# A four-layer message-passing network on one core: the segment maximum worked inside the pipeline of edge phase 2

## The reference

```python
ms = src_s[edge_src] + dst_s[edge_dst]
mv = src_v[edge_src] + dst_v[edge_dst]
w = h @ rw3 + roff
# products of w1..w5 with ms, mv and the edge direction give ds, dv
ls, lv = _eq_lin(ds, dv, lin_ws, lin_bs, lin_wv)
alpha = ls[:, :H * A].reshape(e, H, A)
a = jnp.einsum('ehk,hk->eh', _smooth_leaky(alpha), alpha_dot)      # 8 scores an edge
amax = jax.lax.stop_gradient(jax.ops.segment_max(a, edge_dst, num_segments=n))
a = jnp.exp(a - amax[edge_dst])
a = a / (jax.ops.segment_sum(a, edge_dst, num_segments=n)[edge_dst] + 1e-12)
ns = jax.ops.segment_sum(vs * a[..., None], edge_dst, num_segments=n)
```

## Time and profile before

| | |
|---|---|
| median of 3 runs | 6494.27 us (6494.11 to 6495.6) |
| profiled execution | 6489.29 us, span 6487.5 us |
| PE busy | 5139.3 us (79%) |
| POOL busy | 4415.7 us (68%) |
| DVE busy | 4269.7 us (66%) |
| ACT busy | 2869.0 us (44%) |
| granted TensorE clock | 0.913 of 2.4 GHz |

### The profile page before, as it was taken

The page is one execution under the profiler, slowest core; times in us unless marked ns, Lnnn a source line. Parts: engine busy times, 40 slices in busy tenths (PEclk is TensorE's granted clock), DMA queues, the critical chain, the costliest instruction groups (busy, mean ns, idle before and its releaser), DMA issues. The chain is left out here.

```text
span 6487.5 us, 124927 instructions
## 1 busy us (share of the span) xinstructions
PE 5139.3 (79%) x28257; PEld 3947.1 (61%) x28280; DVE 4269.7 (66%) x14852; ACT 2869.0 (44%) x6302; POOL 4415.7 (68%) x4689
## 2 busy tenths in 40 slices
PE   8899966669997997999655344438999989998676
PEld 6566656646666995677322134337888867776666
DVE  3566658854544886888677521217888878776788
ACT  5333347744443664444200000006777764443566
POOL 8688856658886897766377688875666657887222
PEclk9899989989998998999888766669999999999999
DMA  8566667746665763555311244443333324554665
GB/s 318 126 123 125 121 153 221 220 106 131 130 126 148 232 229 120 166 158 157 115 34 32 76 85 77 74 56 99 110 106 111 105 91 88 88 85 68 223 223 188
DMA packets 592231, 850.72 MB, mean 131 GB/s; under 512 B 220782, under 2 KB 340382, under 8 KB 587566
## 3 DMA queue, kind: packets, MB, share of 16 engines
q1 hardware_dynamic: 409646, 693.65, 33.6%
q0 software_dynamic: 182400, 154.98, 17.3%
HBM read 469.53 MB, written 377.54 MB: 131 GB/s over the span
## 5 line engine op out<-in xcount | busy, mean ns | idle before, releaser
L1140 POOL DMA_INDIRECT xg<-x,gidx x600 | 620.4, 1034 | 250.2 <-issue 184.9
L328 POOL DMA_INDIRECT agg<-summed,cidx x400 | 643.4, 1608 | 194.4 <-issue 113.6
L2017 PE MATMUL pc_a<-msg_a,same_a 128*128 128x168 f32 x1000 | 263.0, 450 | 411.9 <-ACT summed_a L2004 357.8
L2017 PEld LDWEIGHTS pc_a<-msg_a,same_a 128*128 128x128 f32 x1000 | 249.7, 305 | 425.8 <-issue 298.0
L401 DVE TENSOR_TENSOR pr<-pf,ws 128x512 f32<-128x512 f32 x200 | 138.3, 691 | 523.2 <-PE pf L488 399.7
L1151 POOL DMA_INDIRECT agg<-summed,cidx x200 | 322.7, 1613 | 79.7 <-issue 58.5
L1963 POOL DMA_INDIRECT agg<-summed_a,cidx_a x200 | 318.7, 1593 | 70.7 <-issue 59.7
L1314 ACT ACTIVATE ob<-po 128x416 f32<-128x416 f32 (+1 forms) x400 | 201.6, 504 | 359.8 <-PE po L1391 185.7
L1883 PE MATMUL pm_m<-arow_m,ones_m 128*128 128x512 bf16 x400 | 150.9, 466 | 236.7 <-DVE top_m L1830 234.6
L517 PEld LDWEIGHTS pc<-ob,same 128*128 128x128 f32 x2000 | 278.6, 190 | 79.5 <-issue 78.3
L2199 POOL TENSOR_TENSOR rs_n<-ve_n,wsb 128x4 f32<-128x4 f32 x98 | 98.7, 1007 | 333.8 <-DVE nm_n L2187 331.8
(11 more groups left out here) (354 smaller groups left out, 17754.1 us busy)
## 6 DMA issues: line engine op xcount, KB each, us to landing
ar_n<-agg SPq DMA_DIRECT2D x194, 322.0 KB
agg<-zero SPq DMA_DIRECT2D x50, 768.0 KB
ar_n<-agg SPq DMA_DIRECT2D x97, 384.0 KB
agg<-zero SPq DMA_DIRECT2D x50, 672.0 KB
ar_n<-agg SPq DMA_DIRECT2D x97, 336.0 KB
agg<-zero_h SPq DMA_DIRECT2D x25, 1288.0 KB, 5.4
agg<-zero SPq DMA_DIRECT2D x50, 644.0 KB
x<-xn_n SPq DMA_DIRECT2D x97, 324.0 KB, 2.7
```

Of the source, the lines that this page charges most:

```text
L328: pool.indirect_dma_start(agg, bass.IndirectOffsetOnAxis(ap=cidx[r][:, t:t + 1], axis=0), summed[u][:, t, :], None, compute_op=ALU.add).th ...
L1140: pool.indirect_dma_start(xg[s][r][:, t, 0:XR], None, x, bass.IndirectOffsetOnAxis(ap=gidx[s][r][:, t:t + 1], axis=0)).then_inc(gathered[r ...
L2017: last = pe.matmul(pc[:, t, 0:W], same[u][:, s, t * P:(t + 1) * P], msg[u][:, s, :], start=(s == t), stop=(s == T - 1))
```

## The change

Edge phase 2 gets a function of its own, `edge_phase_2`, which also does the maximum; `attention_max_phase` goes. The scores are taken from `val` in SBUF. A unit of spreading is now four heads of a tile in one PSUM bank (eight units a block, two buffers), since PSUM has eight banks for both stages' work: `pt` has two banks in place of three, and the turned scores share bank 1 with the middle group of `turn_rows`; `ph` has one in place of two. The filling of the tables stands ahead of the first gather. The largest lag is 9. The join of the four tables is a stage of its own, `maximum_joined`. `edge_phase_23` is called for layer 3 only. Unchanged are the functions of phase 2 that are not shown, but for their place in the order.

```diff
-def attention_max_phase(nc, dram, mx, wt):
+def edge_phase_2(nc, x, dram, wt, later, yn, mx):
...
-        pa = ps("pa", [3 * H, B])
-        pm = each(3, ps, "pm", [P, H, P])
...
+        pt = ps("pt", [P, 2, B])
+        ph = ps("ph", [P, B])
+        pf = ps("pf", [P, B])
+        po = ps("po", [P, 2, 512])
+        pm = each(2, ps, "pm", [P, 4, P])
...
+        def long_pipeline(eng, stages):
+            pipeline(eng, NB, 4 * R, stages)
...
+            def load_late(i, r, k, parts):
+                sp.wait_ge(w_ps, due(3 * (i - 3)))
+                fence(sp)
+                sp.dma_start(esT[r][0:64], dram["hid"][bass.ds(i * 64, 64)]).then_inc(late[r], 16)
...
+            def keep(i, r, k, parts):
+                u = r % 2
+                sp.wait_ge(val_ok, 3 * (i + 1))
+                fence(sp)
+                sp.wait_ge(vs_ok, i + 1)
+                fence(sp)
+                sp.dma_start(dram["val"][bass.ds(i, 1)].rearrange("a p t c -> (a p) t c"), val[u][:]).then_inc(kept[u], 16)
...
+            def clear_next(i, r, k, parts):
+                w = ZS * AW[3]
+                flat = later.rearrange("(p r) c -> p (r c)", p=P)
+                sp.dma_start(flat[:, bass.ds(i * w, w)], zero[:]).then_inc(cleared, 16)
...
             def to_row(i, r, k, parts):
                 u = r % 2
                 sp.wait_ge(attT_ok, i + 1)
                 fence(sp)
-                sp.wait_ge(m_ps, due(T * (i - 1)))
+                sp.wait_ge(m_ps, due(NU * (i - 1)))
                 fence(sp)
                 sp.dma_start(arow[u][0:3], attT[u][:]).then_inc(row_in[u], 16)
...
-            edge_pipeline(sp, ((3, to_row), (0, load), (4, load_late)))
...
+            long_pipeline(sp, ((0, load), (4, load_late), (5, load_targets), (8, load_midx), (7, keep), (7, to_row), (8, clear_next)))
...
-            edge_pipeline(pool, ((6, send), (5, fetch)))
...
+            pool.memset(low[:], -1e30).then_inc(low_ok, 1)
+            pool.memset(zero[:], 0.0).then_inc(zset, 1)
+            pool.wait_ge(low_out, 16 * T)
+            long_pipeline(pool, ((9, fetch), (0, gather), (9, send)))
...
+                v.wait_ge(sl_ok, i + 1)
+                v.scalar_tensor_tensor(sm[:], o[:, :, SO:SO + 64], 0.25, sl[:], ALU.mult, ALU.add).then_inc(msg_v, 1)
...
+                v.wait_ge(kept[u], 16 * (2 * k + r // 2))
+                v.wait_ge(split_ok, due(7 * (i - 1)))
+                v.tensor_tensor(val[u][:, :, 64:160], vec, m2[:], ALU.add).then_inc(val_ok, 1)
+                v.tensor_tensor(sm[:], sm[:], wt("adot").unsqueeze(1).to_broadcast([P, T, 64]), ALU.mult).then_inc(val_ok, 1)
+                v.wait_ge(val_ok, 3 * i + 2)
+                v.tensor_reduce(val[u][:, :, 160:168], sm[:].rearrange("p t (h k) -> p t h k", k=8), AX.X, ALU.add).then_inc(val_ok, 1)
...
+                    v.wait_ge(m_ps, NU * i + n + 1)
+                    v.tensor_reduce(top[r % 2][:, t, h:h + 4], pm[n % 2][:], AX.X, ALU.max).then_inc(top_ok, 1)
...
+            def with_table(i, r, k, parts):
+                u = r % 2
+                for t in range(T):
+                    v.wait_ge(top_ok, NU * i + 2 * t + 2)
                     v.wait_ge(old_in[t], 16 * (i + 1))
                     v.wait_ge(sent[t], due(16 * (i - 1)))
...
-            edge_pipeline(v, ((5, with_table(0)), (4, largest(0)), (5, with_table(1)), (4, largest(1)),
-                              (5, with_table(2)), (4, largest(2)), (5, with_table(3)), (4, largest(3)), (1, split), (2, targets)))
...
+            long_pipeline(v, ((9, largest(0)), (9, largest(1)), (4, weigh(0)), (9, largest(2)), (2, make_rows(0)), (9, largest(3)), (4, weigh(1)), (9, largest(4)),
+                              (2, make_rows(1)), (9, largest(5)), (4, weigh(2)), (9, largest(6)), (9, largest(7)), (9, with_table), (6, messages), (6, split), (7, targets)))
...
+            def copies(g):
+                def f(i, r, k, parts):
+                    a.wait_ge(f_ps, due(2 * (i - 1)))
+                    a.wait_ge(turned, NG * i + g + 1)
+                    a.activation(ts[r % 2][:, g, :], pt[:, g % 2, :], ACT.Copy).then_inc(ts_ok, 1)
+                return f
...
+            def silu(i, r, k, parts):
+                u = r % 2
+                a.wait_ge(ob_ok, T * (i + 1))
+                a.wait_ge(val_ok, 3 * i)
...
-            edge_pipeline(a, ((2, copied),))
...
+            long_pipeline(a, ((4, weights(0)), (5, outputs(0, 1)), (4, weights(1)), (4, weights(2)), (3, copies(0)), (5, outputs(2, 3)), (5, silu),
+                              (3, copies(1)), (3, copies(2)), (7, scores)))
...
+            def turn_rows(g):
+                def f(i, r, k, parts):
+                    rows, lo = ((xg[0][r], S0), (comb[r % 2], 0), (xg[1][r], S0))[g]
+                    pe.wait_ge(rows_v, (RV * NS * i + RV, RV * (NS * i + 1) + 1, RV * (NS * i + 1) + RV)[g])
+                    if g == 1:
+                        pe.wait_ge(attT_ok, due(i - 4))
+                    else:
+                        pe.wait_ge(ts_ok, NG * i + min(g, 1))
+                    fence(pe)
+                    for t in range(T):
+                        last = pe.transpose(pt[:, g % 2, t * P:(t + 1) * P], rows[:, t, lo:lo + P], wt("ident"))
+                    last.then_inc(turned, 1)
...
+            def turn_scores(i, r, k, parts):
                 pe.wait_ge(split_ok, 7 * (i + 1))
+                pe.wait_ge(ts_ok, upto(NG * (i + 4) + 2, NG * NB))
...
+                    last = pe.transpose(pt[0:3 * H, 1, t * P:(t + 1) * P], three[r % 2][:, t].rearrange("p j h -> p (j h)"), wt("ident"))
+                last.then_inc(att_ps, 1)
...
+            def weights(g):
+                def f(i, r, k, parts):
+                    pe.wait_ge(late[r], 16 * (k + 1))
+                    pe.wait_ge(w_ok, 3 * i + g)
+                    pe.matmul(ph[:], wt(f"w{g + 1}_2"), esT[r][:], start=True, stop=True).then_inc(w_ps, 1)
+                return f
...
+            def spread(n):
+                t, h = n // 2, 4 * (n % 2)
+
+                def f(i, r, k, parts):
+                    u = r % 2
+                    pe.wait_ge(row_in[u], 16 * (2 * k + r // 2 + 1))
+                    pe.wait_ge(ap_ok, T * (i + 1))
+                    pe.wait_ge(top_ok, due(NU * i + n - 1))
                     fence(pe)
-                    for h in (0, 4):
...
+                    pe.matmul(pm[n % 2][:], ones[:], arow[u][:, h:h + 4, t * P:(t + 1) * P], start=True, stop=False)
+                    pe.matmul(pm[n % 2][:], apart[u][:, t, :], diag[:], start=False, stop=True).then_inc(m_ps, 1)
...
-            edge_pipeline(pe, ((4, spread), (2, turn_rows)))
...
+            long_pipeline(pe, ((9, spread(2)), (4, weights(0)), (4, transformed(0)), (9, spread(3)), (5, outputs(0, 1)), (9, spread(4)), (4, weights(1)), (4, transformed(1)),
+                               (9, spread(5)), (4, weights(2)), (3, turn_rows(0)), (9, spread(6)), (5, outputs(2, 3)), (3, turn_rows(1)), (9, spread(7)), (3, turn_rows(2)),
+                               (7, turn_scores), (8, spread(0)), (8, spread(1))))
...
+def maximum_joined(nc, mx):
...
+            for t in range(T):
+                sp.dma_start(part[t][:], flat[t]).then_inc(part_in[t], 16)
+            sp.wait_ge(joined, T - 1)
+            sp.dma_start(flat[0], part[0][:]).then_inc(stored, 16)
+            sp.wait_ge(stored, 16)
...
+            v.wait_ge(part_in[0], 16)
+            for t in range(1, T):
+                v.wait_ge(part_in[t], 16)
+                v.wait_ge(joined, t - 1)
+                v.tensor_tensor(part[0][:], part[0][:], part[t][:], ALU.max).then_inc(joined, 1)
...
-        edge_phase_23(nc, 2, xs[2], None, dram, wt, agg[3], ylen[:, 0, 0:NBP * T])
-        attention_max_phase(nc, dram, mx, wt)
+        edge_phase_2(nc, xs[2], dram, wt, agg[3], ylen[:, 0, 0:NBP * T], mx)
+        maximum_joined(nc, mx)
```

More of the change, by code:

```diff
@@ L1685, in attention_max_phase @@
         diag = sb("diag", [P, 4, P], BF16)
-        part = each(T, sb, "part", [P, NA // P * H])
         tf = sb("tf", [P, T])
@@ L1789, in _ @@
             for u in range(2):
[L1790 to L1793 removed]
+                v.memset(arow[u][:], 0.0).then_inc(ones_ok, 1)
+            v.memset(ones[:], 0.0).then_inc(ones_ok, 1)
+            v.wait_ge(ones_ok, 3)
+            v.memset(ones[0:3], 1.0).then_inc(ones_ok, 1)
             v.tensor_copy(diag[:], wt("ident").unsqueeze(1).to_broadcast([P, 4, P])).then_inc(diag_ok, 1)
+            for r in range(R):
+                v.memset(esT[r][64:P], 0.0).then_inc(blank, 1)
@@ new lines, in _ @@
+            for u in range(2):
+                v.memset(pr[u][96:P, 2, :], 0.0).then_inc(blank, 1)
+            v.memset(lead[:], 0.0).then_inc(blank, 1)
+            v.wait_ge(blank, R + 3)
+            for r in range(R):
+                v.memset(esT[r][64:65], 1.0).then_inc(blank, 1)
+            v.memset(lead[0:1], 1.0).then_inc(blank, 1)
+            v.wait_ge(b_ps, 1)
```

(45 more changed lines are left out.)

263 lines of the change are left out of this document (185 added, 78 removed).

## The result

The changed kernel takes **6890.1 us** (median of three runs, 6885.1 to 6893.3) against 6494.3: a ratio of **1.0607**, interval 1.0588 to 1.0626, so 6% slower. The prediction was 6845, within 6680 to 6940. The profiled execution has a span of 6888.3 us, 401 more than before's 6487.5.

The account below looks back on a forecast made before the run. Merged steps were taken to be bound by a loop through SP's queue, 28.7 us, 30.0 with clock loss. 291 fixed plus 43 x 30.0 gave 1581 us in place of 1230, +351: 6845 us, range 6680 to 6940.

Parts of the forecast that it names:

- The loop through SP: Merged step: esT, weights, messages, silu, score copy and SP's queue form a closed loop, 30.0 us a step; chance 0.84.
- both clock falls: TensorE drops to 1.2 GHz after each of two idle times a step, costing 0.4 and 2.0 us.
- SP to the issue of esT: SP's queue from score copy to issuing the esT load: 0.2 + 1.3 + 2.9 us a step.
- Landing: Time for the 128 KB esT load to arrive after issue: 2.7 us, upper end 5.4.
- with both: Merged step if TensorE's clock falls after both idle times: 31.1 us, against 28.7 without any clock loss.
- the second: TensorE's idle time before esT: a clock fall costing 2.0 us, at a bit under even odds, counted as +0.9.
- the sum: Merged stage and join: 291 + 43 x 30.0 = 1581 us in place of 1230, +351.
- the fixed part: Start, first and last steps, and the join, outside the 43 full-load steps: 291 us, 20 either way.
- What hides what: Engine use in merged steps: GpSimd busy about 16 us of each, TensorE under 60% busy.
- SP early enough: Rival: esT lands before TensorE asks; VectorE and TensorE alternate, 22.9 to 24.2 us a step, 6511 to 6567; chance 0.08.
- GpSimd bound: Rival: full overlap in the merged stage, GpSimd's 20.9 us a step, -81 us, 6413; chance 0.06.
- The other estimate: esT's transfer by the skill's fit, 2.0 us fixed plus bytes over 436e3 per us: 2.3 us, step 28.3.

Follow-up runs that it names:

- the early load: Changed kernel with SP's load of esT one slot earlier (lag 3 in place of 4): 6818.6 us, 1.0071 of the kernel before; again 6776.0 us, 1.0052.
- The late load: Changed kernel with SP's two target loads issued ahead of the load of esT: 7091.7 us, 1.0530 of the kernel before.
- the moved clear: Changed kernel with SP's 768 KB clearing store issued behind the load of esT instead of ahead of the index loads: 7018.7 us, 1.0382 of the kernel before.
- both edits: Changed kernel with esT loaded one slot earlier and VectorE's messages moved to behind the second reduction: 6974.8 us, 1.0294 of the kernel before.
- the version with all three edits: Changed kernel with esT loaded earlier, messages early on VectorE, and GpSimd's table-fill wait moved to its first fetch: 6896.8 us (1.0242), again 6954.6 us (1.0285).
- the changed kernel again: The changed kernel, unaltered, rerun on the experiments' chips: 7053.6 us against 6738.9 for the kernel before, 1.0467.
- TensorE kept busy: Changed kernel with eight products a step whose result nobody reads, placed where TensorE idles: 7094.6 us, 1.0468 of the kernel before.
- early messages: Changed kernel with VectorE's messages moved from behind the table maxima to behind the second reduction: 7041.2 us, 1.0397 of the kernel before.
- two silu buffers: Changed kernel with esT loaded one slot earlier and two buffers for ScalarE's silu instead of one: 7062.1 us, 1.0445 of the kernel before.

## Why the prediction was right, point by point

- **The loop through SP.** Predicted from the first product with esT to the end of the copy of the scores: 21.6, and 2.4 more with both clock falls, 24.0; measured 3195.32 to 3219.55, 24.2. SP to the issue of esT: predicted 4.4, measured 4.1. Landing: predicted 2.7, measured 2.77. Sum of the step shown: 31.1, the 31.1 of "with both". The means of the 42 steps from 2634.2 are 24.4, 3.6 and 2.7, together 30.7. The path is thus the predicted one, and the early load shows that it sets the step. The late load and the moved clear show that its length counts, though not microsecond for microsecond, because the clock's return shifts with it.
- **The clock.** This is the term that was mis-sized, and its mechanism was not quite the predicted one. I took two falls, one in each idle time, and gave the second a bit under even odds and 0.9 us. In most steps there is one fall, in the first idle time, and the work behind it (3217.9 to 3220.6 and 3222.3 to 3223.3 in the step shown) did not bring the clock back ahead of the wait for esT. The price is paid behind that wait all the same: the first product lasted 2.07 or 2.08 us in all 39 steps. (Of the row from which I read the fall I wrote "with nothing busy"; TensorE was idle in it, VectorE and GpSimd were not.) The mean step is 30.7 instead of 30.0. Over 43 steps that is 30 of the 46 us by which the two stages and the join miss the sum (1627 for 1581). The other 16 are the fixed part: 1627 - 43 x 30.7 = 307 for 291, inside the 20 allowed.
- **A part of the nearness is luck.** The 0.7 us of the step are the sum of two errors of opposite sign: the part with the clock was 24.4 for 22.9, that of SP 3.6 for 4.4.
- **What hides what.** GpSimd is busy 16.0 us of each step, as said (521.45 in 1000 us); TensorE 64%, not under 60: at the lower level its products last longer, 2.07 us for 1.02.
- **The rivals.** "SP early enough" did not happen, but its price, 22.9 to 24.2 us a step, is what the early load shows without gathers, 23.9 to 24.6. "GpSimd bound" at 20.9 would need both edits at least. With them the step was 20.0 us where GpSimd had no gathers, and 32.5 in the median, so no run shows it.
- **The landing.** I took 2.7 and kept 5.4. The ring-order rule of the Trainium skill put it near 4: right where the clear is just ahead (3.7), not in the full step, where 2.9 us lie between. The other estimate, 2.3 us, is nearest to the load with nothing large just ahead of it, 2.49 us from issue to product. The Trainium skill ("DMA: Bandwidth & Descriptors", "Anatomy of one DMA") gives that fit for transfers issued by GpSimd, while SP issues this one.

## What to carry to other kernels

When a stage is merged into another's pipeline, follow each queue past every step that moves: a load asked for in the slot that uses it is harmless only as long as nothing in front of it in the queue waits for the same step. Set loads one slot ahead of their use before anything else; here that was one number and 278 us, nearly half of it, by the steps without gathers, through the clock that the wait had kept low. Between a wait that is cured and the time that it should give lies the next wait in line, so read the timeline again after each edit, in a stretch where nothing else disturbs.

## What the runs showed of the hardware

On the three chips of the experiments VectorE and ScalarE stood idle together at the end of long bursts of indirect DMAs from GpSimd. From the version with all three edits, around one burst (3305.67 to 3326.2 us):

```profile
3312.34 0.52 ACT L2041 ACTIVATE ob<-po 128x416 f32<-128x416 f32 x1 [2.14 <-PE po L2123]
3320.92 0.52 ACT L2041 ACTIVATE ob<-po 128x416 f32<-128x416 f32 x1 [8.06 <-DMA x<-xn_n]
3325.82 0.60 ACT L2030 ACTIVATE ws<-ph 128x512 f32<-128x512 f32 x1 [4.38 <-remote]
...
3328.66 0.69 DVE L1938 TENSOR_TENSOR pr<-pf,ws 128x512 f32<-128x512 f32 x1 [11.53 <-DMA x<-xn_n]
```

The second copy waits only for TensorE's tile, whose last product has its record at 3313.03; the copy starts at 3320.92. The named releaser cannot be right: that store belongs to another stage. VectorE resumes 2.4 us after GpSimd's last gather of the burst. Such gaps are in the kernel before as well when it is profiled on such a chip, one of 4.58 us ahead of a reduction in its maximum phase:

```profile
3507.25 0.98 POOL L1781 DMA_INDIRECT mx<-new_m,gidx_m  x1 [0.30 <-issue]
...
3509.40 1.23 DVE L1830 TENSOR_REDUCE top_m<-pm_m 128x8 f32<-128x1024 f32 x1 [4.58 <-issue]
```

There VectorE waits over 3.5 us ahead of 29 of the 200 reductions of the maximum phase, and 189 us ahead of all of them together. In the first profile of the kernel before the longest is 2.5 us and the sum 23 us, though GpSimd hardly pauses there in the maximum phase. The changed kernel in its first timing fits: its step is 30.7 us with gathers and 30.3 and 30.5 without.

The table above fits as well. Where GpSimd's bursts (pauses under 1.2 us counted in) have a mean of 10 us, as in the changed kernel again, esT early or late, clear behind and TensorE kept busy, the median step with gathers is 2.5 to 5.9 us above the one without. In the versions with early messages or two silu buffers, with bursts of 16 to 20 us in the mean, it is 9.3 to 12.5 above. So a larger loss goes with sends, fetches and gathers in one piece; that the bursts cause it was not tested. What it is that makes ScalarE and VectorE resume so late, why it is so in these runs and not in the first timing, and whether the version with both edits would beat 6494 us there, is not settled. The records of TensorE's signals are incomplete in these traces (of the 400 signals behind the spreading, the trace of the version with all three edits has 282), and no run took the gathers or the table stores away alone.
